# The third layer's last expert step with one half block, its columns divided over TensorE's two column halves

## What is computed

```python
x = x + L0_ffn(cond(x, ...)); x = x + L1_ffn(cond(x, ...))
x = x + L2_ffn(cond(x, ...)); x = x + L3_ffn(cond(x, ...))

def _L2_ffn_ref(hidden_states, gate_weight, gate_up_proj, down_proj):
    B, S, H, I, E, K = (4, 256, 256, 512, 8, 2)
...
    probs = softmax(x @ gate_weight.T)
    top_v, top_i = jax.lax.top_k(probs, top_k)
    top_v = top_v / top_v.sum(axis=-1, keepdims=True)
...
    def expert_step(acc, inp):
        gu, dp, w = inp
        gate, up = jnp.split(x @ gu.T, 2, axis=-1)
        hidden = jax.nn.silu(gate) * up
        y = hidden @ dp.T
        return (acc + w[:, None] * y, None)
```

## Time and profile before

| | |
|---|---|
| median of 3 runs | 439.57 us (438.61 to 441.46) |
| profiled execution: its time, its span | 440.36 us, 438.6 us |
| mean granted TensorE clock | 0.976 |
| PE busy | 391.0 us, 89% of the span |
| DVE, POOL, ACT busy | 75%, 57%, 53% |
| the 20 steps of the third layer | about 248 to 380 us |

### The profile page before, as it was taken

One profiled execution on the slowest core, in us unless ns is written; L12 is line 12 of the kernel. 1 busy time (PEld: TensorE's weight loads), 2 busy tenths in 40 slices (PEclk: granted clock), 3 DMA queues, 4 the chain that ended last, 5 costly groups with the idle time before them and its releaser, 6 DMA issues.

```text
span 438.6 us, 6847 instructions
## 1 busy us (share of the span) xinstructions
PE 391.0 (89%) x2027; PEld 244.1 (56%) x2027; DVE 327.2 (75%) x617; ACT 233.7 (53%) x463; POOL 249.0 (57%) x346
## 2 busy tenths in 40 slices
PE   7798999999899999976894999999999999876895
PEld 7676788555455555644673445545554554563463
DVE  5998788999999999989878357744853741058993
ACT  6624593466667766757884422332232233259792
POOL 5475018489678998323840655785687366124641
PEclk9999999999999999998996799999999999999998
DMA  7910005455465645239211377918857510240011
GB/s 208 416 53 0 1 1 174 152 191 177 163 231 195 219 153 171 108 101 369 109 49 48 110 263 260 388 49 297 302 194 233 224 37 25 78 140 0 24 37 36
DMA packets 27363, 65.64 MB, mean 150 GB/s; under 512 B 3360, under 2 KB 7840, under 8 KB 26688
## 3 DMA queue, kind: packets, MB, share of 16 engines
q1 hardware_dynamic: 24320, 58.93, 38.6%
q0 software_dynamic: 1920, 5.25, 3.8%
q10 hardware_dynamic: 1088, 1.05, 0.7%
HBM read 104.40 MB, written 4.85 MB: 249 GB/s over the span
## 4 chain that ended last, share of the span: by engine, by line
PE 53%; DVE 29%; issue 9%; ACT 5%; POOL 2%; DMA 2%; SPq 0%; DVEq 0%; POOLq 0%; ACTq 0%
PE bank L2019 16%; PE bank L2040 9%; PE bank L1795 5%; DVE hx L1320 4%; DVE fw L1109 4%; DVE bw L1112 3%; PE bank L1640 3%; PE bank L2030 3%; PE bank L1641 3%; PE bank L1642 3%; DVE fw L1117 2%; PE bank L1892 2%; PE bank L1717 2%; PE bank L1878 2%; DVE gl L1599 2%
## 5 line engine op out<-in xcount | busy, mean ns | idle before, releaser
L2019 PE MATMUL bank<-gu,xbT 128*64 128x512 f32 x320 | 72.9, 594 | 0.9 <-ACT xbT L945 0.9
L1795 PE MATMUL bank<-hx,w2raw 128*128 128x512 f32 x128 | 67.3, 607 | 4.7 <-DVE hx L1320 3.9
L833 ACT ACTIVATE rl<-bank 128x512 f32<-128x512 f32 x64 | 38.1, 595 | 38.7 <-PE bank L1642 37.9
L1535 DVE TENSOR_TENSOR hm<-bank,sl 128x512 f32<-128x512 f32 x20 | 13.8, 689 | 50.8 <-issue 32.2
L1640 PE MATMUL bank<-xlhi,w1hi 128*128 128x512 f32 x64 | 49.3, 771 | 0.0
L2019 PEld LDWEIGHTS bank<-gu,xbT 128*64 128x64 f32 x320 | 25.8, 137 | 34.7 <-issue 30.0
L1320 DVE TENSOR_TENSOR hx<-bank,cwb 128x512 f32<-128x512 f32 x64 | 42.2, 662 | 3.1 <-ACT bank L837 3.0
L2040 PE MATMUL bank<-dn,hT 128*64 128x256 f32 x320 | 38.9, 384 | 3.0 <-ACT hT L956 0.7
L1117 DVE RECIPROCAL fw<-fw 128x256 f32<-128x256 f32 x23 | 39.8, 1732 | 0.0
L837 ACT ACTIVATE bank<-rl 128x512 f32<-128x512 f32 x64 | 38.1, 596 | 0.0
L614 POOL DMA_INDIRECT y_rows<-yb,dest_i x20 | 22.5, 1125 | 25.9 <-ACT yb L962 25.0
(11 more groups left out here) (305 smaller groups left out, 909.4 us busy)
## 6 DMA issues: line engine op xcount, KB each, us to landing
gu<-in_gu SPq DMA_DIRECT2D x88, 512.0 KB
dn<-in_dn SPq DMA_DIRECT2D x44, 512.0 KB
cwb<-cw_rows SPq DMA_DIRECT2D x32, 512.0 KB, 3.8
traw<-in_t SPq DMA_DIRECT2D x3, 1024.0 KB, 7.2
w1raw<-in_w SPq DMA_DIRECT2D x8, 256.0 KB, 4.6
w2raw<-in_w SPq DMA_DIRECT2D x8, 256.0 KB, 4.3
kT<-in_kt SPq DMA_DIRECT2D x4, 256.0 KB, 5.0
x<-in_x SPq DMA_DIRECT2D x2, 512.0 KB, 6.9
```

The costliest lines, as they stand in the source:

```text
L833: act.activation(rl[:, u % 3, :], bank[u % 4][:], ACT.Relu).then_inc(sem("r_ready"), 1)
L1795: pe.matmul(bank[4 + s][:], w2raw[:, e // 4 % 2, e % 4, :], hx[:, 0, u % 4, :], start=(e == 0), stop=(e == E0 - 1), skip_group_check=True) ...
L2019: ins = pe.matmul(bank[2 * (b % 2) + up][part(g), :], xbT[:, b % 2, k, part(g)], gu[:, 2 * g + b % 2, k, up * I2:up * I2 + I2], start=(k = ...
```

## The change

Step 19 (`END`) handles slab 19 alone, on all 128 partitions: the table of slab numbers says 19 in its 40th place too, so both halves gather the same 64 rows. Partitions 0 to 63 take the first 256 of the gate's and of the up's 512 columns, partitions 64 to 127 the other 256. Silu and product are half as wide, there are two transposes for four and one copy of them for two, the down matmuls sum four chunks into 128 output columns on each half of the partitions, the copy to `yb` is 128 wide, and the scatter writes half rows of 512 bytes, by a table `end_i` of its own. The second half's conditional weight loads of step 19 go. Three small DVE instructions and one small POOL instruction are new.

```diff
+END = NB - 1
+        def inner(b):
+            return slice(0, I2 // 2 if b == END else I2)
+        def halves(b):
+            return range(1 if b == END else 2)
...
# SP
+            def groups(b):
+                return range(1 if b == END else GROUPS)
-                    for g in range(GROUPS):
+                    for g in groups(b):          (owners, up_weights, down_weights)
# POOL
-                pool.iota(slab[:], [[1, NH]], base=0, channel_multiplier=0, **kw).then_inc(sem("route_consts"), 1)
+                pool.iota(slab[:, 0:NH - 1], [[1, NH - 1]], base=0, channel_multiplier=0, **kw).then_inc(sem("route_consts"), 1)
+                pool.memset(slab[:, NH - 1:NH], float(END)).then_inc(sem("route_consts"), 1)
...
-                pool.indirect_dma_start(y_d, bass.IndirectOffsetOnAxis(ap=dest_i[:, b:b + 1], axis=0), yb[:, b % 2, :], None
-                                        ).then_inc(sem(f"y_out{b % 2}"), 16)
+                if b == END:
+                    rows, to, of = y_d.rearrange("r (h c) -> (r h) c", h=2), end_i[:], yb[:, b % 2, 0:C // 2]
+                else:
+                    rows, to, of = y_d, dest_i[:, b:b + 1], yb[:, b % 2, :]
+                pool.indirect_dma_start(rows, bass.IndirectOffsetOnAxis(ap=to, axis=0), of, None).then_inc(sem(f"y_out{b % 2}"), 16)
# ACT
+                n = inner(b)
-                act.activation(sl[:, b % 2, :], bank[2 * (b % 2)][:], ACT.Silu).then_inc(sem("sl_ready"), 1)
+                act.activation(sl[:, b % 2, n], bank[2 * (b % 2)][:, n], ACT.Silu).then_inc(sem("sl_ready"), 1)
...
-                act.activation(yb[:, b % 2, :], y_bank(b), ACT.Copy).then_inc(sem("y_ready"), 1)
+                n = slice(0, C // 2 if b == END else C)
+                act.activation(yb[:, b % 2, n], y_bank(b)[:, n], ACT.Copy).then_inc(sem("y_ready"), 1)
...
-                    hidden_turned(b - 1, 0)
-                    hidden_turned(b - 1, 1)
+                    for half in halves(b - 1):
+                        hidden_turned(b - 1, half)
# DVE
+            dve.tensor_scalar(row_f[:, 3, 1:2], part_no[:], float(PART), None, ALU.is_gt)
+            chain(dve.scalar_tensor_tensor(out=row_f[:, 3, 0:1], in0=row_f[:, 1, END:NB], scalar=-1.0, in1=row_f[:, 2, END:NB],
+                                           op0=ALU.add, op1=ALU.add))
+            chain(dve.scalar_tensor_tensor(out=end_i[:], in0=row_f[:, 3, 0:1], scalar=2.0, in1=row_f[:, 3, 1:2],
+                                           op0=ALU.mult, op1=ALU.add))
...
+                n = inner(b)
+                dve.tensor_tensor(hm[:, b % 2, n], bank[2 * (b % 2) + 1][:, n], sl[:, b % 2, n], ALU.mult).then_inc(sem("hm_ready"), 1)
# PE
-                            ins = pe.matmul(bank[2 * (b % 2) + up][part(g), :], xbT[:, b % 2, k, part(g)],
-                                            gu[:, 2 * g + b % 2, k, up * I2:up * I2 + I2], start=(k == 0), stop=(k == KC - 1))
+                            if b == END:
+                                n = up * I2 + g * (I2 // 2)
+                                rhs = gu[:, b % 2, k, n:n + I2 // 2]
+                            else:
+                                rhs = gu[:, 2 * g + b % 2, k, up * I2:up * I2 + I2]
+                            ins = pe.matmul(bank[2 * (b % 2) + up][part(g), inner(b)], xbT[:, b % 2, k, part(g)], rhs,
+                                            start=(k == 0), stop=(k == KC - 1))
...
-                for half in range(2):
+                for half in halves(b):
...
+            def end_down(b):
+                pe.wait_ge(sem("hT2_ready"), 2 * b + 1)
+                for c in range(4):
+                    for half in range(GROUPS):
+                        n = slice(half * (C // 2), half * (C // 2) + C // 2)
+                        ins = pe.matmul(y_bank(b)[part(half), 0:C // 2], hT2[:, b % 2, c % 2, part(c // 2)], dn[:, b % 2, c, n],
+                                        start=(c == 0), stop=(c == 3))
+                ins.then_inc(sem("d_done"), 1)
```

More of the change, by code:

```diff
@@ L46 @@
 FULL = TOK // PART
+END = NB - 1
+assert (TOP2 * TOK + E2 * (PART - 1)) // PART < NH
 HALF_NAME = ("gate", "up")
@@ L222, in build @@
         dest_i = sb("dest_i", [P, NB], I32)
+        end_i = sb("end_i", [P, 1], I32)
         cw2p = sb("cw2p", [P, 2, NT])
@@ L384, in owners @@
             def owners(b):
-                for g in range(GROUPS):
+                for g in groups(b):
                     h = NB * g + b
                     owner[h] = sp.value_load(owner_i[h:h + 1, 0:1], min_val=0, max_val=E2 - 1)
+            def groups(b):
+                return range(1 if b == END else GROUPS)
             def held(b, g):
@@ L477, in route_consts @@
                 pool.memset(starts[:, 0, 0:1], 0.0).then_inc(sem("route_consts"), 1)
-                pool.wait_ge(sem("route_consts"), 12)
+                pool.wait_ge(sem("route_consts"), 13)
                 pool.tensor_scalar(lane[:], lane[:], -1.0 / PART, 0.0, ALU.mult, ALU.add).then_inc(sem("route_consts"), 1)
@@ L1439, in per_token @@
                 return r2[:, i, :, 0:1].to_broadcast([P, NT, E2])
-            dve.wait_ge(sem("route_consts"), 15)
+            dve.wait_ge(sem("route_consts"), 16)
             sq = [r2c[:, i, :, :].rearrange("p t (g h) -> p t g h", g=E2) for i in range(2)]
@@ L1534, in block_h @@
                 wait(dve, sem("ht_ready"), 2 * b - 2)
-                dve.tensor_tensor(hm[:, b % 2, :], bank[2 * (b % 2) + 1][:], sl[:, b % 2, :], ALU.mult).then_inc(sem("hm_ready"), 1)
+                n = inner(b)
+                dve.tensor_tensor(hm[:, b % 2, n], bank[2 * (b % 2) + 1][:, n], sl[:, b % 2, n], ALU.mult).then_inc(sem("hm_ready"), 1)
             def late_scan(i, part):
@@ L1961, in _ @@
             logits(3)
-            pe.wait_ge(sem("route_consts"), 15)
+            pe.wait_ge(sem("route_consts"), 16)
             pe.wait_ge(sem("routed"), ROUTED["mk"])
@@ L2005, in turn_block, with weights_in @@
                 ins.then_inc(sem("xbt_ready"), 1)
+            def weights_in(b):
+                return 16 * GROUPS * (b // 2 + 2) - (16 if b == END else 0)
             def gate_up(b):
@@ L2013, in gate_up @@
                 for up in range(2):
-                    pe.wait_ge(sem(f"{HALF_NAME[up]}_in{b % 2}"), 16 * GROUPS * (b // 2 + 2))
+                    pe.wait_ge(sem(f"{HALF_NAME[up]}_in{b % 2}"), weights_in(b))
                     if up and b in (4, 10, 16):
@@ L2031, in turn_block_hidden @@
                     ins.then_inc(sem("ht_ready"), 1)
+            def end_down(b):
[6 more added lines that the diff above has]
+                ins.then_inc(sem("d_done"), 1)
             def block_down(b):
-                pe.wait_ge(sem(f"dn_in{b % 2}"), 16 * GROUPS * (b // 2 + 2))
+                pe.wait_ge(sem(f"dn_in{b % 2}"), weights_in(b))
                 wait(pe, sem("y_ready"), b)
+                if b == END:
+                    end_down(b)
+                    return
                 for j in range(4):
```

## The result

The changed kernel takes 437.17 us (median of 6 runs, 435.68 to 438.29) against 439.95 us for the kernel before beside it (6 runs). The ratio is 0.9927, with a 95% interval of 0.9907 to 0.9948: 0.7% faster, 2.3 to 4.1 us of 440. Forecast were 437.0 us and 2.6 us less than before.

The account below looks back on a forecast made before the run. PE bounds the kernel, with step 19 on the path up to its scatter's landing. The terms 1.68 + 0.70 + 0.11 + 0.10 = 2.59 us take the median from 439.57 to 437.0 us, range 435.4 to 439.6.

Parts of the forecast that it names:

- Where the time is: Step 19 lies on the path from its first matmul to its scatter's landing; savings there move everything behind them.
- Gate and up: Step 19 on PE: 16 instructions of 256 columns instead of 512, 3.43 to 1.75 us, saving 1.68 us.
- the 1.75 named as the sign: Expected in the changed profile: step 19's 16 gate and up instructions take about 1.75 us to the next group's start.
- ACT's silu: Step 19's silu, ahead of the copy of step 18's turned product, would not come too late; cover 0.8 us.
- The link: Transposes and copy between the down products of steps 18 and 19: half goes, but PE's wait stays; counted at nothing.
- Down product: Step 19 on PE: sixteen instructions of 128 columns instead of 256, 0.109 to 0.065 us each, saving 0.70 us.
- Copy and scatter: Step 19's copy to `yb` at 128 columns saves 0.11 us; its scatter of half rows saves 0.10 us.
- What was added: Three DVE instructions, some 0.6 us, and a POOL memset, 0.11 us, fall in idle time and cost nothing.
- The sign named for it: Expected in the changed profile: the first step's start stays where it was.
- Rival one: Step 19's column halves hinder each other on PE; only copy and scatter save, 0.2 us, 439.4 us; chance 0.12.
- Rival two: Clock falls in PE's gap before the adding of the rows, which takes 7.4 us: 1.1 slower, 440.7; chance 0.05.
- The forecast of 1.4 for it: PE's wait before the adding of the rows shortens from 1.63 us to 1.4 us.

Follow-up runs that it names:

- the two repeated-column variants: The changed kernel with step 19's gate and up columns, or its down product's columns, streamed twice, the second results unread: 438.53 us and 437.69 us.

## Why the prediction was right, step by step

- **Where the time is.** That step 19 lies on the path from its first matmul to the landing of its scatter, and that the rest follows, was right: what the two repeated-column variants put back (1.70 and 0.85 us) reaches the start of the row load in full, and the runs show 2.0 and 1.0 us, the second with overlapping intervals. Counted from the start of step 18's gate and up, the adding of the rows starts 2.60 us earlier (20.07 for 22.67) in the first profile and 2.86 in the second; that the first is just the 2.6 forecast is luck, 2.84 less a row load that was 0.24 longer.
- **Gate and up:** 1.68 forecast, 1.70 measured in the chain. The down product's form gave the price of the new one to 0.02 us. The forecast set a chain piece (3.43) against a time from start to start (1.75). Like against like it is 3.43 - 1.73 in the chain and 3.56 - 1.85 from first start to the next group's, so the mixing did no harm, but the 1.75 named as the sign is 1.85.
- **ACT's silu** did not hold back step 18's transposes. It ran from 369.73 for 0.38, and the copy that follows it waited for PE until 370.96; the forecast cover was 0.8 us, the idle time before that copy is 0.85.
- **The link**, counted at nothing: 1.0 us in both.
- **Down product:** 0.70 forecast, 0.85 measured, near the upper bound of 0.88. This is the term that was mis-sized. From its start to the next group's are 375.39 - 374.37 = 1.02 us, 0.064 for each instruction; I took 0.065 for each, but set it against 16 x 0.109 = 1.75, where the row of before reads 377.36 - 375.48 = 1.88 from start to start. The 0.095 us a weight load that gave the lower bound is not a floor: 16 loads kept the loader busy for 0.88 us here, 0.055 each, and 1.52 before. Whether the loads or the columns set the 0.064 is not shown. The Trainium skill's 81 ns for a matmul with its load at 128 columns ("TensorE: Matmul & The Clock Gate", "Back-to-back issue gap") does not hold for this form: 64 ns an instruction.
- **Copy and scatter:** 0.11 and 0.10 forecast, 0.10 and 0.17 measured. The scatter lost what half the bytes were worth in the rows; half rows cost no more than whole ones. What the Trainium skill says of 512 B ("DMA: Bandwidth & Descriptors", "Specifications") agrees as far as 512 B go: 2.24 us to the landing, for 2.41 with rows of 1024 B. No run has a shorter row.
- **What was added** cost nothing that can be seen: the fourth layer's first scan starts at 244.84 us behind the three new DVE rows, and DVE is then idle for 6.28 us. The sign named for it, the first step's start, can't be read this finely: gate and up of step 0 start at 248.62 us in the changed kernel's first profile and 247.59 in its second, 248.38 before.
- **Rival one** (halves that don't run side by side) is refuted by the 1.73 us for gate and up and the 1.11 for the down product. **Rival two** (the clock falls in the gap) too: the gap was 1.59 us, 1.33 the second time, at a clock of 1.00 in both, and the adding of the rows still takes 3.71 us. The forecast of 1.4 for it fits only to 0.2 us, since the row load varies by 0.26.
- **The clock** does fall, but at the end of the fourth layer and in both kernels. I had put the 2.85 us between the runs of before down to chance; a part of it, 1.5 us in an execution in which it falls, is this; another is the start of step 19, which moves by up to 1.4 us between the profiles (367.28 to 368.69).

The sum of the terms was 2.6 us against 2.84 in the traces, near the upper end of the 1.4 to 2.9 that the terms allowed. The 0.08 for the copy in the lower bound stands there without a working; the copy measured 0.10. That the median came out at 437.17 for 437.0 is partly luck, since the kernel before took 439.95 beside it and not the 439.57 that the forecast started from. The runs give 2.3 to 4.1 us, which holds both. Whether the runs' middle, 3.2 us, has something in it beyond the 2.84 can't be told with these intervals.

## What to carry to other kernels

Where the last pass of a pipeline is half empty, as here, its cost is latency at the join with the next stage, and it is priced by the rows of the same instruction form elsewhere in the trace. Dividing the columns of the one live block over both halves of the array takes that cost down where PE is on the path, and a half step may be ready early enough to move ahead of the work of the step before it. A change of under 1% is read from an interval between two places in the program, since spans of single executions differ by more for reasons of their own: 3.1 us between the two profiles of the changed kernel, whose intervals differ by 0.01.

## What the runs showed of the hardware that was not expected

- The granted clock can fall at the end of one execution and not of the next of the same program (54.2 or 52.7 us for the fourth layer, 1.5 us), after a stretch in which PE was busy for 0.58 us of 2; after one of 0.52 of 2 in another variant it did not fall. With six unused matmuls in that stretch it stayed at 1.00 in both profiles, and the runs of the kernel before spread over 1.6 us for 3.3.
- Matmuls of this form (f32, 64-wide weights on alternating column halves) go at 0.214, 0.109 and 0.064 us an instruction for 512, 256 and 128 moving columns at a granted clock of 1.00: about in proportion down to 256, with 0.01 us above it at 128.
